# Adapted MoE-LoRA kernel, stage of batch 0: the next batch's x transposed on VectorE, and W transposed through two PSUM banks

## The reference

```
# layer 0: a LoRA adapter, gathered by batch
Bx  = einsum('bni,bri->bnr', x, B0[adapter_ids])        # rank 16
x   = x + einsum('bnr,bor->bno', Bx, A0[adapter_ids])
# layer 1: a dense product and 8 gated LoRA experts, top 2 of 8
base   = einsum('btd,od->bto', x, W)                    # W is 2048 x 2048
logits = einsum('btd,ed->bte', x, Wr) + 5.0 * one_hot(language)
gates  = softmax over the two largest logits, 0 for the others
h      = einsum('btd,erd->bter', x, A)
x      = x + base + 2.0 * einsum('bter,bte,eor->bto', h, gates, Bm)
```

## Time and profile before

| | |
|---|---|
| runs shown | 1623.5, 1625.05, 1627.42 us; median 1625.05 us |
| the profiled execution's own time | 1623.4 us |
| its span | 1621.6 us (1.8 us of its time lie around the span) |
| TensorE busy / weight loads | 1587.1 us (98%) / 1336.5 us (82%) |
| VectorE / ScalarE busy | 1176.2 us (73%) / 758.7 us (47%) |
| DMA | 351.30 MB, mean 217 GB/s |
| stage of batch 0 | from 77 us to 338.5 us of the span |

### The profile page before, as it was taken

The page is one execution under the profiler, slowest core; times in us unless marked ns, Lnnn a source line. Parts: engine busy times, 40 slices in busy tenths (PEclk is TensorE's granted clock), DMA queues, the critical chain, the costliest instruction groups (busy, mean ns, idle before and its releaser), DMA issues.

```text
span 1621.6 us, 21156 instructions
## 1 busy us (share of the span) xinstructions
PE 1587.1 (98%) x7744; PEld 1336.5 (82%) x7744; DVE 1176.2 (73%) x1599; ACT 758.7 (47%) x1000; POOL 9.8 (1%) x19
## 2 busy tenths in 40 slices
PE   7799999999999999999999999999999999999998
PEld 5687888788888888888888888888888888888887
DVE  3575444687778976888768876888769877787665
ACT  4553344344544554455444554445544544445443
POOL 1000000000000000000000000000000000000000
PEclk9899999999999999999999999999999999999999
DMA  8689797879886887879977797878877788576665
GB/s 240 190 214 252 211 241 188 214 220 239 204 220 220 220 218 197 233 224 230 219 200 230 217 232 191 234 223 224 214 200 233 222 227 205 195 234 207 207 217 161
DMA packets 396985, 351.30 MB, mean 217 GB/s; under 512 B 250522, under 2 KB 323530, under 8 KB 395850
## 3 DMA queue, kind: packets, MB, share of 16 engines
q1 hardware_dynamic: 394706, 345.76, 77.5%
q10 hardware_dynamic: 2176, 4.19, 0.9%
HBM read 280.62 MB, written 68.82 MB: 215 GB/s over the span
## 4 chain that ended last, share of the span: by engine, by line
PE 93%; DMA 2%; ACT 1%; SPq 1%; DVE 1%; issue 1%; ACTq 0%; DVEq 0%
PE pb L746 27%; PE pb L747 27%; PE pb L748 27%; PE pb L366 4%; PE pb L368 3%; PE pb L514 2%; PE pb L649 1%; SPq L625 1%; PE pb L314 1%; DMA raw<-in_L_cond_W_dram 1%; DMA wrn<-in_L_cond_Wr_dram 1%; ACT xah L342 0%; DMA t_scr<-raw 0%; DMA t_scr<-tst 0%; DMA bt_scr<-bt 0%
## 5 line engine op out<-in xcount | busy, mean ns | idle before, releaser
L742 DVE TENSOR_TENSOR wl<-raw,wh 128x1024 fp32r<-128x1024 f32 (+1 forms) x456 | 555.1, 1217 | 333.9 <-ACT wh L738 333.7
L738 ACT CAST wh<-raw 128x1024 fp32r<-128x1024 f32 (+1 forms) x456 | 477.1, 1046 | 683.7 <-PE pb L748 675.6
L746 PE MATMUL pb<-wh,sh 128*128 128x512 f32 x1568 | 612.8, 391 | 0.5 <-DVE ost L782 0.5
L747 PE MATMUL pb<-wl,sh 128*128 128x512 f32 x1568 | 611.6, 390 | 0.0
L748 PE MATMUL pb<-wh,sl 128*128 128x512 f32 x1568 | 611.2, 390 | 0.0
L748 PEld LDWEIGHTS pb<-wh,sl 128*128 128x128 f32 x1568 | 294.3, 188 | 62.8
L746 PEld LDWEIGHTS pb<-wh,sh 128*128 128x128 f32 x1568 | 294.6, 188 | 56.2 <-DVE wl L742 0.9
L747 PEld LDWEIGHTS pb<-wl,sh 128*128 128x128 f32 x1568 | 294.6, 188 | 55.0
L366 PE MATMUL pb<-awb,xah 128*128 128x304 f32 x512 | 138.4, 304 | 2.9 <-DVE aux L381 1.6
L368 PE MATMUL pb<-awb,xal 128*128 128x256 f32 x512 | 134.4, 280 | 0.0
L746 PE MATMUL pb<-wh,xh 128*128 128x512 f32 x256 | 106.2, 415 | 1.2 <-DVE ost L782 0.8
(11 more groups left out here) (135 smaller groups left out, 1280.6 us busy)
## 6 DMA issues: line engine op xcount, KB each, us to landing
raw<-t_scr SPq DMA_DIRECT2D x392, 512.0 KB, 4.4
xst<-in_x_dram SPq DMA_DIRECT2D x768, 32.0 KB, 3.7
raw<-in_L_cond_W_dram SPq DMA_DIRECT2D x128, 128.0 KB, 3.9
t_scr<-tst SPq DMA_DIRECT2D x32, 512.0 KB, 5.1
raw<-bt_scr SPq DMA_DIRECT2D x28, 512.0 KB, 3.9
out_dram<-ost SPq DMA_DIRECT2D x28, 512.0 KB, 4.4
out_dram<-u SPq DMA_DIRECT2D x28, 512.0 KB, 3.4
t_scr<-raw SPq DMA_DIRECT2D x32, 256.0 KB, 4.1
```

Of the source, the lines that this page charges most:

```text
L738: e.copy(pair_split(wh, g), pair_source(g)).then_inc(c_wh, 1)
L742: e.tensor_tensor(out=pair_split(wl, g), in0=pair_source(g), in1=pair_split(wh, g).bitcast(f32), op=ALU.subtract).then_inc(c_wl, 1)
L746: e.matmul(o, h, wh[:, g % RING, k, :], start=start, stop=False)
L747: e.matmul(o, h, wl[:, g % RING, k, :], start=False, stop=False)
```

## The change

1. x of batch 1 is loaded in the order `x_b`, 16 DMAs per m, 128 in all, of 32 KB each: eight per slot in SP's slots 4 to 7 and 10 to 21. It is transposed by `x_turn` at the head of VectorE's slots 9 to 24. The TensorE transposes and ScalarE copies of batch 1 are gone.
2. The halves of W go to banks 6 + h. Each waits for the copy of the same half of the block before.
3. Bank 6 is thus taken. In batch 0 `bx_transpose` and `hg_transpose` use bank 5, deltas 0 to 5 banks 4 and 5, deltas 6 to 15 bank 4 alone. `bx_transpose(1)` uses bank 5, deltas of batch 1 alternate between banks 4 and 5.
4. The first delta of slots 1, 2 and 3 goes to the head of TensorE's slot. Of the second wait conditions, `bt_transpose(0)` waits for delta 5's addition, delta 12 for `aux_final(0)`.

```diff
         def x_load(e, n, m, parts=range(4)):
             half, cols = m // 4, m % 4
             if n == 0:
                 if m >= 4:
                     e.wait_ge(c_tr, 2 * m - 6)
-            elif n == 1 and m < 2:
-                e.wait_ge(c_bt, 4)
...
-            if n < 2:
-                e.dma_start(x_place(n, m), x_v[n, half, :, :, cols * CW:(cols + 1) * CW])\
-                 .then_inc(d_x[m % 2] if n else d_x0[m % 4], 16)
-            else:
+                e.dma_start(x_place(m), x_v[0, half, :, :, cols * CW:(cols + 1) * CW]).then_inc(d_x0[m % 4], 16)
+            else:
+                if n == 1 and m < 2:
+                    e.wait_ge(c_bt, 4)
+                elif 0 in parts:
+                    e.wait_ge(c_xc, 16 * n + 2 * m - 2)
                 for a in parts:
                     for k in range(4):
                         e.dma_start(x_block(m)[32 * a:32 * a + 32, :, k, :], x_b[n, half, cols, k, a])\
                          .then_inc(d_x[m % 2], 16)
...
         def delta_bank(n, u):
             if n == 0:
-                return 6 if u >= 12 or u % 2 == 0 else 4
-            return (6, 4, 5)[u % 3] if n == 1 else x_bank(n, u)
+                return 4 + u % 2 if u < 6 else 4
+            return 4 + u % 2 if n == 1 else 6 + u % 2
...
         def w_transpose(e, g, h):
...
-            if w or h:
-                e.wait_ge(c_wc, 2 * w + h)
+            if w:
+                e.wait_ge(c_wc, 2 * w + h - 1)
             else:
                 e.wait_ge(c_xc, 16)
             for j in range(4):
-                last = e.transpose(pb[:, 7, j * P:(j + 1) * P], w_raw(g)[:, j, h, :], ident[:, :])
+                last = e.transpose(pb[:, 6 + h, j * P:(j + 1) * P], w_raw(g)[:, j, h, :], ident[:, :])
...
         def pe_main(e):
             for i in range(SLOTS0):
...
-                if i in (5, 6):
-                    delta(e, 0, 2 * i + 3)
+                if i and i in DELTAS0 and i != 4:
+                    delta(e, 0, DELTAS0[i][0])
...
-                if 9 <= i < 25:
-                    x_transpose(e, 1, i - 9)
...
         def act_main(e):
...
-                if 9 <= i < 25:
-                    x_keep(e, 1, i - 9)
...
         def dve_main(e):
             for i in range(SLOTS0):
+                if 9 <= i < 25:
+                    x_turn(e, 1, i - 9)
                 pair_lo(e, i + 2)
...
         def sp_main(e):
...
-                if i in (4, 5):
-                    x_load(e, 1, i - 4)
-                if i in range(11, 22, 2):
-                    x_load(e, 1, (i - 7) // 2)
+                if 4 <= i < 8:
+                    x_load(e, 1, (i - 4) // 2, (i % 2 * 2, i % 2 * 2 + 1))
+                if 10 <= i < 22:
+                    x_load(e, 1, (i - 6) // 2, (i % 2 * 2, i % 2 * 2 + 1))
```

More of the change, by code:

```diff
@@ L250, in x_turn @@
             if u % 2 == 0:
-                e.wait_ge(d_x[m % 2], 64 + 256 * (4 * (n - 2) + m // 2 + 1))
+                e.wait_ge(d_x[m % 2], 256 * (4 * (n - 1) + m // 2 + 1))
             if kp == 0:
                 b = n - 1
-                if q < 2:
+                if n == 1:
+                    e.wait_ge(c_l0, 16)
+                elif q < 2:
                     if n == 2:
@@ L313, in x_transpose, with x_keep @@
                     at = (u % 2 * 2 + k) * P
-                    last = e.transpose(pb[:, x_bank(n, u), (2 * k + t) * P:(2 * k + t + 1) * P],
-                                       x_place(n, m)[:, t, at:at + P], ident[:, :])
+                    last = e.transpose(pb[:, 6 + u % 2, (2 * k + t) * P:(2 * k + t + 1) * P],
+                                       x_place(m)[:, t, at:at + P], ident[:, :])
             last.then_inc(c_tr, 1)
-        def x_keep(e, n, u):
+        def x_keep(e, u):
             q, kp = x_unit(u)
[L320 to L333, removed]
+            e.wait_ge(c_tr, u + 1)
+            e.copy(two(0, q, kp), pb[:, 6 + u % 2, :]).then_inc(c_xc, 1)
         def x_hi(e, n, u):
@@ L392, in bx_lo, with bx_bank, hg_bank @@
              .then_inc(c_gd, 1)
+        def bx_bank(n):
+            return 5 if n < 2 else 6
+        def hg_bank(n):
+            return 6 if n else 5
         def bx_transpose(e, n):
@@ L397, in bx_transpose @@
             for t in range(TT):
-                last = e.transpose(pb[:, 6, t * P:(t + 1) * P], st48[:, t, :], ident[:, :])
+                last = e.transpose(pb[:, bx_bank(n), t * P:(t + 1) * P], st48[:, t, :], ident[:, :])
             last.then_inc(c_gp, 1)
@@ L404, in bx_keep @@
                 e.wait_ge(c_dl, 16 * n)
-            e.copy(bxt[:, :], pb[:, 6, :]).then_inc(c_ga, 1)
+            e.copy(bxt[:, :], pb[:, bx_bank(n), :]).then_inc(c_ga, 1)
         def aux_adapted(e, n):
@@ L470, in hg_transpose @@
             e.wait_ge(c_x1, 16 * n + 16)
+            if n == 1:
+                e.wait_ge(c_wc, 64)
             for t in range(TT):
-                last = e.transpose(pb[:, 6, t * P:(t + 1) * P], hg[:, t, :], ident[:, :])
+                last = e.transpose(pb[:, hg_bank(n), t * P:(t + 1) * P], hg[:, t, :], ident[:, :])
             last.then_inc(c_gp, 1)
@@ L480, in hg_hi @@
                 e.wait_ge(d_btd, 16)
-            e.copy(hgh[:, :], pb[:, 6, :]).then_inc(c_ga, 1)
+            e.copy(hgh[:, :], pb[:, hg_bank(n), :]).then_inc(c_ga, 1)
         def hg_lo(e, n):
             e.wait_ge(c_ga, GA * n + 7)
-            e.tensor_tensor(out=hgl[:, :], in0=pb[:, 6, :], in1=hgh[:, :].bitcast(f32), op=ALU.subtract)\
+            e.tensor_tensor(out=hgl[:, :], in0=pb[:, hg_bank(n), :], in1=hgh[:, :].bitcast(f32), op=ALU.subtract)\
              .then_inc(c_gd, 1)
@@ L502, in delta @@
                     e.wait_ge(d_ar, 48)
[L503 to L506, removed]
+            if n == 0 and u == 12:
+                e.wait_ge(c_gd, 5)
+            if n == 1 and u < 2:
                 e.wait_ge(c_gd, GD * n + 5)
-            elif n == 1:
-                e.wait_ge(c_x1, 16 * n + u - 2)
             elif u >= 2:
-                e.wait_ge(c_x1, 16 * n + u - 1)
+                e.wait_ge(c_x1, u if n == 0 and u >= 7 else 16 * n + u - 1)
             for k in range(2):
@@ L659, in w_keep @@
             e.wait_ge(c_wt, 2 * w + h + 1)
-            e.copy(w_kept(g)[:, h, :], pb[:, 7, :]).then_inc(c_wc, 1)
+            e.copy(w_kept(g)[:, h, :], pb[:, 6 + h, :]).then_inc(c_wc, 1)
         def w_sums(e, g):
@@ L1089, in pe_start @@
             for u in range(2, 4):
[L1090 removed]
+                x_transpose(e, u)
             for s in range(12):
[L1092 removed]
+                x_transpose(e, 4 + s)
                 aux_products(e, 0, s)
@@ L1284, in pe_main @@
                 for u in DELTAS0.get(i, ()):
-                    if u not in (13, 15):
+                    if i == 0 or i == 4 or u > DELTAS0[i][0]:
                         delta(e, 0, u)
```

45 lines of the change are left out of this document (14 added, 31 removed).

## The result

The changed kernel takes 1641.23 us (median of 4 runs, 1640.91 to 1641.76); the kernel before took 1624.82 us in the runs beside it. The ratio is 1.0099, 95% interval 1.0082 to 1.0117: 16.4 us slower. The profiled execution has a span of 1639.3 us, 17.7 us over that of before. The forecast was 1632, slower by 7.

The account below looks back on a forecast made before the run. TensorE was full, and the added x issues would make SP's queue the bound of slots 7 to 23. 8.5 - 1.2 - 0.8 + 0.9 = +7.4 us gave 1632 us, range 1617 to 1642.

Parts of the forecast that it names:

- the three small terms: Two banks at the start -1.2 us, the early first delta -0.8, the clock's fall after slot 9's wait +0.9.
- rival A: SP's queue bounds slots 7 to 23, the forecast itself: 1626 to 1641 us, chance 0.6.
- rival B: In SP's slots 10 to 21 the issues fit, TensorE keeps its 7.0 us: 1616 us, partly 1618 to 1621; chance 0.23.
- the number at the head of slot 9: Block 12's load moves from 137.27 to about 141.5; TensorE gets it at about 148.7, 4.0 us later.
- Moved past: w_store and the next w_sums_store go 4.2 us later behind x loads; ScalarE's w_keep is late, covered by the two banks.
- the failed step: Slots 10 to 21: SP slots of 8.35 us, 98.5 in all after credits, 83.0 for slots 10 to 19; +4.4 us.
- `x_turn`'s wait for x: On VectorE: x, issued two slots ahead, lands 3.7 us after issue, 6.1 at worst, so the wait should be nil.
- The deltas of batch 1: Three deltas per slot on two banks in place of three: 0 to 1 us, taken as 0.
- Start and early deltas: Two banks at the start of W gain 1.2 us (0 to 1.8); the early first delta gains 0.8 (0 to 0.9).
- The clock: Half speed after a wait of some 4 us at slot 9: 0 to 1.7 us lost, taken as +0.9.
- Rival C: The DMA engines are the bound, share about 0.95, W's loads land later: 1638 to 1645 us, chance 0.07.
- Rival D: Gain and loss cancel: SP's slots about 7.7 us, slot 9's wait 1.5 us; 1622 to 1628 us, chance 0.10.

Follow-up runs that it names:

- x_on_act: The changed kernel with all 128 loads of x for batch 1 issued by ScalarE's queue instead of SP's: 1625.9 us, 0.9998 of the kernel before.
- half_x_loads: The changed kernel with half of batch 1's x loads left out, four issues per slot on SP in place of eight: 1622.8 us, ratio 0.9990.
- late_x_on_sp: start_and_deltas with batch 1's x changed from its third block on, 96 loads on SP, W in two banks from block 16 to 31: 1633.9 us, ratio 1.0054.
- late_x_on_act: late_x_on_sp with the 96 loads on ScalarE's queue: 1619.4 us, 0.9970 of the kernel before.
- late_banks: The changed kernel with blocks of W from 32 in bank 7 alone and deltas of batch 1 in banks 6, 4, 5: 1642.9 us, ratio 1.0111.
- start_and_deltas: The kernel before with W's first three blocks through banks 6 and 7, bx_transpose(0) in bank 5, early first deltas in slots 1 to 3: 1623.6 us, 0.9987.
- x_on_pool: The changed kernel with all 128 loads of x for batch 1 on GpSimd, with their own semaphores: 1628.1 us, 1.0012 of the kernel before.
- one_bank: The changed kernel with both halves of W again in bank 7, each waiting for the copy of the half before: 1644.8 us, ratio 1.0114.

## Why the prediction was right in kind and too small by more than half

**The sum.** The forecast was +7.4 us, the profile shows +17.7. Of the 10.3 us between them 7.3 arise ahead of slot 22. 1.1 are the three small terms (-1.2, -0.8, +0.9): the forecast start of slot 22 leaves them out, the measured one has whatever became of them. The other 1.9 lie behind slot 22, where -0.3 was forecast and 1.6 measured. The time, 1641.2 us, is still at the top of rival A's own range (1626 to 1641), but by luck: that top stood for SP slots of 9.0 us through slower W issues, and most slots took 8.3 (8.65 on average).

**SP's queue is the bound (rival A): right for slots 10 to 21, shown by x_on_act, half_x_loads and the pair late_x_on_sp, late_x_on_act.** The price of an x issue was put at 0.53 us; it was 0.495 in undisturbed groups. The rule weighed there, from the Trainium skill's page "DMA: Bandwidth & Descriptors", section "Issuing engines are not separate DMA queues", that initiating a DMA is usually small beside the DMA itself, agrees with the trace for a single load: 0.495 us of the queue beside a median of 3.6 us to its landing. It does not lead to rival B's 1616, for eight of them are 4.0 us of one queue in every slot. The section on the anatomy of a DMA, also weighed there, describes the path of DMAs that GpSimd issues; these are SP's.

**TensorE gains 7.0 us: right in the main.** With no x loads slots 10 to 21 take 87.6 us, 4.6 less than before; 5.3 were forecast. The whole floor is 1616.1, and that rival B's sum gave 1616 is chance: the floor's profile has 3.7 us less than before in slots 0 to 9, where only one of the 16 units was transposed, and 1.3 more in slots 22 to 35.

**Slots 0 to 9: the number at the head of slot 9 was right, but only one of its two reasons was seen, and what followed was wrong.** Block 12's load was forecast for 141.5 and began at 141.13; TensorE was to get it at 148.7 and started on it at 148.89:

```profile
148.89 1.08 PE L626 MATMUL pb<-ident,raw 128*128 128x128 f32 x4 [6.51 <-DVE raw L612]
```

But VectorE's addition stands behind its sums of block 10, and these had waited for the landing of the sums' store before them. They end where the addition begins, at 148.29:

```profile
146.70 0.42 DVE L646 TENSOR_TENSOR tst<-raw 128x256 f32<-128x256 f32 x1 [5.58 <-DMA t_scr<-tst]
148.29 0.49 DVE L612 TENSOR_TENSOR raw<-raw,ident 128x128 f32<-128x128 f32 x2
```

The last of block 12's loads landed at 148.3 too, 4.9 us after its issue. So two chains end together there and the forecast had one: a quicker load alone would have won nothing. Slot 10 began at 158.1, not at 156.6: slot 9 took 8.5 us, its first half 5.7 at a granted clock of 0.54 (3.2 at the full clock). SP's slot 10 came at 164.7 instead of 162.75. It has no x loads ahead of it; it waited 2.4 us for the sums, which had waited for the store of the sums before, itself late (156.34):

```profile
163.12 0.43 DVE L646 TENSOR_TENSOR tst<-raw 128x256 f32<-128x256 f32 x1 [2.79 <-DMA t_scr<-tst]
```

The step "Moved past", which put this store behind x loads, counted only ScalarE's wait, not this ring of store, landing and sums on a single buffer. Nor is SP's queue the whole of it: on ScalarE or GpSimd these slots took 79.2 to 79.9 us, against 71.5 with no x loads. In x_on_act one wait of 3.2 us of that is ScalarE's own; what the rest comes from, the full DMA engines (a share of 1.00 from 130 to 148 us in x_on_act) or the order of the loads, no run separates.

**Slots 10 to 21: the failed step.** It said slots of 8.35 us, *less* 1.2, 1.0 and 0.9 us for slots 12, 14 and 15, which have fewer issues, and 2.6 more for slot 17: 83.0 us from slot 10 to slot 20. 86.9 were measured, 3.9 more. The plain slots up to 16 took 8.05 to 8.34 us, as forecast. The credits did not come, which is 3.3 us: slot 12 took 8.30, slot 14 8.70 and slot 15 8.28. Slots 17 to 19 took 1.0 us more than forecast, in 18 and 19 with W's loads at 3.0 us for four, and slots 10, 11, 13 and 16 0.5 less. In slots 12 and 15 fewer issues ahead only made the next x loads longer (5.08 and 5.18 in place of 3.92).

In slot 14 SP stood still for 2.3 us, waiting for `pair_lo`. Here another step failed: `x_turn`'s wait for x, forecast to be nil, is 11.2 us in six waits, 4.5 at the longest. It was one of the prediction's own signs of being wrong. VectorE's turn of slot 15 waits for the x that SP issued late, `pair_lo` stands behind it, and SP's next load of W behind that:

```profile
199.12 0.71 DVE L264 STREAM_TRANSPOSE pool_a<-xst 128x512 f32<-128x512 f32 x1 [1.88 <-DMA xst<-in_x_dram]
199.76 0.65 DVE L719 TENSOR_TENSOR wl<-raw,wh 128x512 fp32r<-128x512 f32 x1
200.44 1.92 SPq L602 DMA_DIRECT2D raw<-in_L_cond_W_dram  x4
```

And slot 22 was to begin 7.4 us after SP's slot 20 (block 25 landing after 7.1); it began 8.9 us after it, on this wait:

```profile
260.04 0.65 PE L626 MATMUL pb<-ident,raw 128*128 128x128 f32 x4 [1.13 <-DMA raw<-in_L_cond_W_dram]
```

So slot 22 began at 260.5 and not at 253.2. The 7.3 us are 1.9 (SP's slot 10), 3.9 (SP's slots 10 to 19) and 1.5 (landing).

**The deltas of batch 1: costed at nothing, worth up to 2.5 us.** I looked at the number of banks and not at what bank 4 holds. The first delta now waits for `aux_final(1)` at the head of slot 29:

```profile
310.31 0.48 PE L491 MATMUL pb<-bxt,a0g 128*128 128x256 f32 x2 [3.09 <-DVE aux L399]
```

Slots 28 to 35 took 55.3 us for 52.8. late_banks took that wait out and its time did not fall, so what it is worth in the total is not shown.

**Start and early deltas:** forecast 2.0 together, measured 2.4 (start_and_deltas). **The clock:** 0.9 us was added, 1.7 at most. The fall at slot 9 cost that slot 2.5 us; whether any of it reaches the end is not shown, for SP's slot 10 hung on the store of the sums. **Rival C** falls for slots 10 to 21 (share 0.98 with 88.2 us) and stays open for slots 0 to 9. **Rival D** did not occur.

## What to carry to other kernels

Count issues per slot of the queue as one counts instructions of an engine, and compare the sum with the slot: in slots 10 to 21 they were free below it (four x loads, 0 us), and above it each slot ran at the queue's pace (eight, 14.8 us in twelve slots). Don't credit a saturated queue with slots that have a little less to issue. When a store or a load is moved to a later place, look for the ring that it closes: who waits for its landing, and what stands behind that wait. When the work is moved off a full engine, ask which queue pays, and give it to the one with room: 96 of the 128 loads on ScalarE's queue in slots 10 to 21, with the first two blocks left as they were, turned +16 us into -5.

## What the runs showed of the hardware

- An issue of 256 pieces of 128 bytes took 0.45 us on SP's queue (median; 0.495 from start to start in a row of eight), 0.47 on ScalarE's (x_on_act) and 0.58 on GpSimd's (x_on_pool). The sums' store of 512 KB returned in 0.45 us, but the four W loads behind it took 2.84 us (at 173.25), in place of 1.99 with no store ahead (at 206.36) and 1.92 with 2.3 us between (at 200.44): part of its cost shows in the issues that follow.
- The DMA engines' share reached 0.98 to 1.01 over some 90 us with TensorE almost free of waits (x_on_act, late_x_on_act). A share of 0.91 was no sign of room, nor was 0.98 a sign of a bound.
- In the changed kernel the granted clock fell to half (1.2 GHz) in or just behind TensorE's waits of 2.45, 2.68, 3.27, 4.11 and 6.51 us in slots 6 to 20. The length of one wait does not decide it: behind a wait of 1.13 us it fell at slot 0 (75.66) and stayed full at slot 22 (260.04), and in one_bank it stayed full behind a wait of 3.00 us (126.50).
